# Packed register words for loop addresses, and one more tile of each group weighted by VectorE

## The reference, cut to what matters

```python
Q = (enh @ Wq + bq).reshape(N, H, D)          # N = 3125 nodes, H = 4, D = 64
K = (enh @ Wk + bk).reshape(N, H, D)
V = (enh @ Wv + bv).reshape(N, H, D)
rel = rel_w[edge_relations]
mod_k = K[src] + 0.2 * rel[:, None, :]
scores = jnp.einsum('ehd,ehd->eh', Q[dst], mod_k) / D ** 0.5
seg_max = jax.ops.segment_max(scores, dst, num_segments=N)
ex = jnp.exp(scores - seg_max[dst])
denom = jax.ops.segment_sum(ex, dst, num_segments=N)
w = ex / denom[dst]
agg = jax.ops.segment_sum(w[:, :, None] * V[src], dst, num_segments=N)
```

## Time and profile before

| what | before |
|---|---|
| median of three runs | 1229.86 us (1229.55 to 1232.69) |
| profiled execution, own time | 1231.86 us |
| its span | 1230.0 us |
| mean granted clock of TensorE | 0.935 |
| busy share PE / DVE / ACT / POOL | 84% / 72% / 66% / 64% |

### The profile page before, as it was taken

The page is one execution under the profiler, slowest core; times in us unless marked ns, Lnnn a source line. Parts: engine busy times, 40 slices in busy tenths (PEclk is TensorE's granted clock), DMA queues, the critical chain, the costliest instruction groups (busy, mean ns, idle before and its releaser), DMA issues. The chain is left out here.

```text
span 1230.0 us, 28148 instructions
## 1 busy us (share of the span) xinstructions
PE 1034.3 (84%) x6923; PEld 773.3 (63%) x6924; DVE 883.3 (72%) x1938; ACT 814.8 (66%) x2770; POOL 792.4 (64%) x851
## 2 busy tenths in 40 slices
PE   5899966888888888888888888877998489999993
PEld 3577743555555555555555555544896378999993
DVE  6788547899999898999999998953886823333331
ACT  3344410388888888888888888864677456666772
POOL 3576747777777777777777777602784346666662
PEclk9899975599999999999999999987997689999997
DMA  8233438887788787878778777772425724443445
GB/s 243 87 122 123 140 108 241 249 240 229 225 226 227 219 231 220 232 219 230 224 219 232 219 228 225 204 238 82 155 87 150 246 64 70 71 67 65 69 68 130
DMA packets 125490, 212.92 MB, mean 173 GB/s; under 512 B 22638, under 2 KB 86058, under 8 KB 125044
## 3 DMA queue, kind: packets, MB, share of 16 engines
q0 software_dynamic: 46336, 132.09, 40.5%
q1 hardware_dynamic: 79028, 79.31, 21.2%
HBM read 180.32 MB, written 34.21 MB: 174 GB/s over the span
## 5 line engine op out<-in xcount | busy, mean ns | idle before, releaser
L685 POOL DMA_INDIRECT KV<-kv,SRC x440 | 459.3, 1044 | 166.9 <-issue 91.2
L694 ACT ACTIVATE KV<-KV,WS 128x65 f32<-128x65 f32 x1452 | 387.1, 338 | 64.5 <-issue 61.8
L801 PE MATMUL ps_o<-KV,PM 128*128 128x260 f32 x880 | 272.2, 405 | 7.2 <-ACT KV L694 4.4
L776 PE MATMUL ps_qe<-Q,PT 128*128 x1320 | 206.9, 291 | 59.1 <-issue 40.8
L776 PEld LDWEIGHTS ps_qe<-Q,PT 128*128 128x128 bf16 x1320 | 123.4, 100 | 124.8 <-issue 89.2
L708 ACT COPY ACC<-ps_o x439 | 157.2, 358 | 32.1 <-PE ps_o L801 24.6
L801 PEld LDWEIGHTS ps_o<-KV,PM 128*128 128x128 f32 x880 | 135.6, 194 | 55.6 <-issue 17.2
L895 DVE TENSOR_TENSOR KV<-KV,ps_qe 128x512 f32<-128x512 f32 x220 | 141.8, 677 | 0.3
L888 DVE TENSOR_TENSOR KV<-KV,ps_u 128x1024 f32<-128x1024 f32 x110 | 132.9, 1208 | 10.1 <-DMA KV<-kv,SRC 9.2
L901 DVE TENSOR_REDUCE S<-KV 128x16 f32<-128x1024 f32 x110 | 132.4, 1204 | 0.9
L1552 POOL DMA_INDIRECT acc<-YG,DX x56 | 88.9, 1587 | 61.0 <-issue 36.6
(11 more groups left out here) (304 smaller groups left out, 1604.3 us busy)
## 6 DMA issues: line engine op xcount, KB each, us to landing
dlb<-dl_rows SPq DMA_DIRECT2D x110, 128.0 KB
tyb<-ty_rows SPq DMA_DIRECT2D x110, 64.0 KB
KV<-kv,SRC POOLq DMA_INDIRECT x440
kv<-kvb SPq DMA_DIRECT2D x25, 258.0 KB, 2.5
xs_rows<-xs SPq DMA_DIRECT2D x25, 256.0 KB, 2.5
KV<-xs_rows SPq DMA_DIRECT2D x10, 640.0 KB, 9.7
Q<-in_f_W_dram SPq DMA_DIRECT2D x8, 512.0 KB, 7.2
KV<-in_f_W_dram SPq DMA_DIRECT2D x8, 512.0 KB, 6.7
```

Of the source, the lines that this page charges most:

```text
L685: pool.indirect_dma_start(kv[:, t % RING, :], None, d["kv"], bass.IndirectOffsetOnAxis(ap=T["SRC"][:, t:t + 1], axis=0)).then_inc(s_g[g % ...
L694: m = a.activation(part, part, ACT.Copy, scale=W[:, t // CB_ % 2, at:at + 1])
L776: m = pe.matmul(T["ps_qe"][:, p % 3, k, :], T["PT"][:, h, (p % 2 * 2 + k) * P:(p % 2 * 2 + k + 1) * P], T["Q3"][:, bass.ds(at[k] + n * C, ...
L801: pe.matmul(ps_o[:, bass.ds(bank, A)], PM[:, g % 2, t % G, :], kv[:, t % RING, C:KVW], start=False, stop=True, skip_group_check=True).then ...
```

## The change

`load_word` loads one integer that holds several small numbers, and `field` takes one of them out in registers: a shift, a mask, a product.

- PE loads two words for a group in place of twelve values in three loads: `query_word` (four blocks of 5 bits) and `place_word` (for each of four tiles its own bank and the bank to be cleared, 2 bits each).
- ACT loads one `copy_word` (for two tiles a bank of 2 bits and a block of 5) where it loaded two pairs of values. DVE's rescale takes its bank from `place_word`.
- In the first phase `query_words`, `bank_numbers`, `copy_words` and `place_words` compute the words; the scaled rows are gone.
- `by_vector` gives DVE the last tile of every group up to the last nine, not of every odd one (51 tiles more); ACT has these no more.
- DVE's `rescale` stands behind `place` and the first `multiply`, where it stood ahead of them.

```diff
+def load_word(nc, engine, ap):
+
+    return nc.values_load_multi_w_load_instructions(ap, engines=(engine,), min_val=0, max_val=(1 << 24) - 1,
+                                                    skip_runtime_bounds_check_because="a word packs fields of node blocks and banks")[1][0]
+
+
+def field(word, low, bits, scale, high):
+
+    part = (word >> low if low else word) & ((1 << bits) - 1)
+    return part.with_bounds(min_val=0, max_val=high) * scale
...
             def block_rows():
                 v.wait_ge(s_sp, 2)
                 blocks = spread[0:1, :, :].rearrange("a k (c p) -> a k c p", c=SC // 2)
-                q(v.tensor_scalar(T["qRow"][0:1, :].rearrange("a (p k c) -> a k c p", k=2, c=SC // 2), blocks, float(3 * C), None, ALU.mult))
-                q(v.tensor_scalar(T["aRow"][0:1, :].rearrange("a (p k c) -> a k c p", k=2, c=SC // 2), blocks, float(A), None, ALU.mult))
...
-            def bank_rows():
...
+            def gather_digits(word, row, n, base):
+
+                digits = row.rearrange("a (g k) -> a g k", k=n)
+                q(v.scalar_tensor_tensor(out=word, in0=digits[:, :, n - 1], scalar=base, in1=digits[:, :, n - 2], op0=ALU.mult, op1=ALU.add))
+                for k in range(n - 3, -1, -1):
+                    q(v.scalar_tensor_tensor(out=word, in0=word, scalar=base, in1=digits[:, :, k], op0=ALU.mult, op1=ALU.add))
+
+            def query_words():
+                word = T["word"][0:1, 0:NG]
+                gather_digits(word, T["bRow"][0:1, :], G, 32.0)
+                q(v.tensor_copy(T["query_word"][0:1, :], word))
+
+            def bank_numbers():
...
+                q(v.scalar_tensor_tensor(out=after, in0=mine, scalar=1.0, in1=third, op0=ALU.add, op1=ALU.add))
+
+            def copy_words():
...
+                gather_digits(T["word"][0:1, :], ahead, 2, 128.0)
+                q(v.tensor_copy(T["copy_word"][0:1, :], T["word"][0:1, :]))
+
+            def place_words():
+
+                mine, after, word = T["mine"][0:1, :], T["after"][0:1, :], T["word"][0:1, 0:NG]
+                q(v.scalar_tensor_tensor(out=mine[:, 1:NS], in0=after[:, 0:NS - 1], scalar=4.0, in1=mine[:, 1:NS], op0=ALU.mult, op1=ALU.add))
+                gather_digits(word, mine, G, 16.0)
+                q(v.tensor_copy(T["place_word"][0:1, :], word))
...
+                if i == 3:
+                    query_words()
                 if i == 4:
-                    bank_rows()
+                    bank_numbers()
+                if i == 5:
+                    copy_words()
+                    place_words()
...
-        return ((3, 1),) if g % 2 else ()
+        return ((3, 1),)
...
-            def before(q):
+            def before(t):
 
-                return (load_values(nc, mybir.EngineType.Activation, T["aRow"][0:1, q:q + 2], (NT - 1) * A),
-                        load_values(nc, mybir.EngineType.Activation, T["last_bank"][0:1, q:q + 2], 2 * 512))
+                i = t // 2
+                word = load_word(nc, mybir.EngineType.Activation, T["copy_word"][0:1, i:i + 1])
+                return ([field(word, 7 * k + 2, 5, A, NT - 1) for k in range(2)], [field(word, 7 * k, 2, 512, RO - 1) for k in range(2)])
...
             def rows(G_):
-                return load_values(nc, mybir.EngineType.PE, T["qRow"][0:1, G * G_:G * G_ + G], (NT - 1) * 3 * C)
-
-            def banks(name, t, n):
-                return load_values(nc, mybir.EngineType.PE, T[name][0:1, t:t + n], 2 * 512)
+                word = load_word(nc, mybir.EngineType.PE, T["query_word"][0:1, G_:G_ + 1])
+                return [field(word, 5 * k, 5, 3 * C, NT - 1) for k in range(G)]
+
+            def banks(g):
+
+                word = load_word(nc, mybir.EngineType.PE, T["place_word"][0:1, g:g + 1])
+                return ([field(word, 4 * k, 2, 512, RO - 1) for k in range(G)], [field(word, 4 * k + 2, 2, 512, RO - 1) for k in range(G)])
...
                 if summed:
-                    own = banks("own_bank", g * G, G)
-                    after = banks("next_bank", max(g * G - 1, 0), G)
-                    shift = 1 if g == 0 else 0
+                    own, after = banks(g)
...
                 t = c * CB_ - 1
-                bank = load_values(nc, mybir.EngineType.DVE, T["own_bank"][0:1, t:t + 1], 2 * 512)[0]
+                g = c * CG - 1
+                bank = field(load_word(nc, mybir.EngineType.DVE, T["place_word"][0:1, g:g + 1]), 4 * (G - 1), 2, 512, RO - 1)
...
-                if g > 0 and g % CG == 0:
-                    rescale(g // CG)
                 if summed:
                     place(g)
...
                     multiply(2 * x)
                 elif summed:
                     weigh(g, *by_vector(g)[0])
+                if g > 0 and g % CG == 0:
+                    rescale(g // CG)
```

## The result

The changed kernel takes 1302.31 us (median of four runs, 1300.57 to 1307.92) beside 1229.7 us of the kernel before in the same comparison: a ratio of 1.0593, 95% interval 1.0554 to 1.0631. It is 5.9% slower; 1299 us was forecast. The profiled execution has a span of 1306.1 us.

A forecast was written before the change was run, and what follows sets the result against it. PE's own instruction queue was taken to bound the kernel. From the profiled 1231.86 us, +68 (period), +1.5 (tail) and 0 (preparation) gave 1301.4, as a median 1299 us; ends 1260 and 1343, range carried down to 1225.

The forecast's parts named there:

- The bound: Steady stretch, period 5.69 us: other engines wait for PE, and PE for its own queue, whose loads take 1.66 us a group.
- The form: Field-taking on PE's queue: 22 shifts and masks as single instructions, 0.10 us each, 2.20 us a group; fused, 0.20 us.
- The queue's sum: PE's queue per group: -1.84 (loads) + 0.72 (words) + 2.20 (shifts, masks) + 0.11 (products) = +1.19 us.
- The cover: Queue time hidden by waits for other engines: 0.14 to 0.88 us a group, middle 0.51; period grows 0.68 us, +68 us.
- The tail: Last ten iterations, after 804 us: PE's queue +0.48 us each, partly behind ACT; +1.5 us (0 to +5).
- Rival B: Shifts and masks fuse, PE's queue 0.81 us shorter, DVE and POOL bind: about 1204 us (1198 to 1225); chance 0.16.
- Weighs and rescale: On DVE: 51 more weighs cost +21 us, the rescale's wait of 21.5 us comes back; nearly cancel.
- the wait ahead of the rescale: DVE's 21.5 us over 18 rescales, 1.2 us each, to be covered by placement and first product; gone in the next profile.
- Rival D: Fields computed anew at each use: queries' 7 instructions become 21, +1.4 us a group, over 1400 us; chance 3 in 100.
- Preparation: First phase, DVE: 7.8 us of operations go, 21 operations of 9 to 10 us come, in gaps: 0 (-1 to +4).
- The chances: Faster 0.17, same 0.03, slower 0.80, with a bound of 0.3%, 3.7 us.
- C: Rival: fields single but cheap (queue -0.31 us a group), or cover takes everything: no change, 1215 to 1240 us; chance 0.05.

The follow-up runs named there:

- e11: Kernel before the change, next banks stored one place later so PE's third load begins at a multiple of four: 1205.1 us, ratio 0.979.
- e5: Changed kernel, but PE loads the four query rows unpacked; banks stay packed: 1235.2 us, ratio 1.004 to the kernel before.
- e6: Changed kernel, but PE loads the eight banks unpacked; queries stay packed: 1260.9 us, ratio 1.025 to the kernel before.
- e3: Changed kernel, but ACT loads its two pairs of values unpacked, as before the change: 1308.0 us, ratio 1.065 to the kernel before.
- e4: Changed kernel, but PE's three loads and DVE's rescale bank unpacked; ACT keeps its word: 1211.3 us, ratio 0.985 to the kernel before.
- e1: Kernel before the change plus the 51 added weighs and the later rescale, without the words: 1225.5 us, ratio 0.998.
- e10: e8, but ACT loads four ready values in one load beginning at a multiple of four, instead of a word: 1179.9 us, ratio 0.958.
- e8: e7, but DVE's placement reads its column numbers from PSUM instead of SBUF: 1194.6 us, ratio 0.971 to the kernel before.
- e2: Changed kernel with the words kept, but weighs and rescale as before the change: 1306.0 us, ratio 1.062 to the kernel before.
- e7: e4, but next banks stored one place later so their load begins at a multiple of four: 1208.9 us, ratio 0.982.
- e9: e8, but DVE weighs the last tile of odd groups only, as before the change: 1184.5 us, ratio 0.963.

## Why the prediction was right

**The bound.** PE's queue was named as what ends the period. e11 shows it: 0.67 us taken from the queue alone, 0.27 us less a group, until the gathers end it (0.305 us of idle time ahead of each, 106.1 / 348).

**The form.** That shifts and masks go as single instructions was a judgement with a chance, since no row showed one; the rows of after show 22 of them a group, as counted. Their price was put at 0.10 us from four rows 0.10 us apart; e5 and e6 give 0.097 to 0.099. The loads: 0.30 us taken, 0.301 and 0.305 found. The queue's sum was +1.19 us; with 0.097 it is +1.12.

**The cover was too large.** 0.51 us of it was to disappear where the queue waits for others, the middle of 0.14 and 0.88. The period rose by 0.81 us, so 1.12 - 0.81 = 0.31 disappeared. In e5 and e6 the same sum leaves 0.32 and 0.31 (0.43 and 0.69 us of queue, 0.11 and 0.38 of period): the cover is used up once, and what comes on top counts in full. The larger bound was made for the most part of "issue" idle time, in which PE waits for its own queue, and that is no cover. Why it is 0.31 and not the 0.14 in which PE waits for DVE was not followed. +0.81 for +0.68 in 100 iterations is some 13 us that the sum lacked.

**The tail had the wrong sign.** +1.5 us was forecast; from the last one-hot to the last copy of sums it takes 50.5 us where it took 54.9: -4.3 us. The step that failed: the tail's term counted PE's queue (+0.48 us an iteration) and put ACT's shorter queue at nothing, "while PE's queue rules". That holds for the steady stretch (the changed kernel and e3 have the same period, 6.51 us), not for the last groups. The changed kernel against e3, e4 against e1 and e10 against e8 show it: there each saving on ACT's queue shortens the tail by 5 to 6 us. Rival B had named such a gain, some 6 us, for its own case only. Between the two profiled executions the sum was +69.5 us, and 1307.92 - 1231.86 = +76.1 came: some 13 too little in the period, 6 too much in the tail. That the median met the forecast so closely is luck to that extent: it lies 5.6 us under the profiled execution, where 2.0 had been taken off.

**Weighs and rescale** were to cancel, and they do while PE's queue binds (e1 is 3 us under the kernel before beside it, e2 4 us over the changed kernel). That the wait ahead of the rescale would be gone is wrong: 15.1 us over 18 in place of 21.5 are left, as PE comes later. It costs nothing, DVE having time.

**Rival B's places were right, and so were its sums for POOL.** With PE's queue out of the way POOL ends the period. B put this at 5.41 us, and at 5.62 if each added weigh holds a gather by its own time; e11, without these weighs, has 5.43, and e7, with them, 5.62 (the two differ in ACT's word too). B's time with contention, near 1222 us, is 13 above e7's 1208.9. e9 against e8 gives 0.11 us a group and not 0.2, as POOL has breaks again there (0.34 us ahead of a gather, 121.4 / 355). **Rival D** (fields anew at each use) is ruled out: the query line has 7 instructions a group, not 21. **Preparation:** 21 operations came where 12 went, and the first one-hot starts at 182.6 us for 181.1; over all kernels here it starts between 175.8 and 183.3, in no order that follows their edits. **The chances:** the parts stated for B and C add up to 0.18 for faster and 0.02 for the same; the 0.17 and 0.03 written down are each off by 0.01.

## What to carry to other kernels

Count an engine's queue as a resource of its own: where "issue" stands ahead of matmuls and the loads' durations are as long as the gap, each register load and each single register instruction there goes into the period at par, beyond a cover that was 0.31 us a group here. The engine's busy share does not tell this bound: PE's array is 82% busy in e6 at 6.08 us (383.96 of 470 us) and 90% in e10 at 5.31. An operation on registers that does not fuse costs a tenth of a us on PE's queue, so a field of a packed word (two of them) is dearer than its share of a load of ready values: four values that begin at a multiple of four cost 0.33 us, one word 0.30. Before packing, look at the minimum of a load's row against its median: 327 against 1003 ns said that some place in the array was the trouble, and moving an array by one element was worth 25 us.

## What was not expected of the hardware

A load of four values goes by where it begins, and two can be dearer than four. PE's load of four values takes 0.33 us from a multiple of four and 1.00 us from the place before one; moving the array alone made the difference (e11). One word takes 0.30 us on PE, and the 110 words of a row, loaded in turn, begin at every place. ACT's load of two values takes 0.48 us or more from odd and from even places, its load of four from a multiple of four 0.308 us. Two values on PE, and four on ACT from another place, were not run. And moving one input of an operation of DVE to PSUM, at the same duration of that operation, made POOL's gathers 0.05 us shorter each and the kernel 14.3 us faster.
